# A cross-attention and mixed feed-forward layer on one core: residual and output sums of GpSimd made one step earlier, statistics and mix ahead of the query rounding on VectorE, query products behind both halves of the scores on TensorE

## The reference, cut to what matters

```python
# block 1: attention with 16 query heads of 16, one shared key/value head
xn = layernorm(x)
q  = (xn @ Wq + bq) -> 16 heads;  k = ctx @ Wk + bk;  v = ctx @ Wv + bv
p  = softmax(where(mask == 0, -1e9, q k^T / 4))
x1 = x + (p v) @ Wo + bo
# block 2: mix along the sequence, nine paths, one chosen per token
x2 = layernorm(x1)
xm = mk[0]*x2[s-1] + mk[1]*x2[s] + mk[2]*x2[s+1]
h  = xm @ W1[p] + b1[p]        (9 paths of 64);   gate = tanh(xm @ Wo1 + bo1) @ Wo2 + bo2
c  = (h[chosen] @ W2[chosen] + b2[chosen]),  chosen = argmax(gate)
out = x1 + layernorm(x2 + c) * gamma + beta
```

## Time and profile before

| what | us |
|---|---|
| median of 3 runs | 396.97 |
| lowest and highest of them | 395.99, 398.92 |
| the profiled execution | 397.85 |
| span of its instructions | 396.0 |
| TensorE busy | 335.4 |
| VectorE busy | 265.0 |
| GpSimd busy | 190.0 |
| ScalarE busy | 182.7 |

### The profile page before, as it was taken

The page is one execution under the profiler, slowest core; times in us unless marked ns, Lnnn a source line. Parts: engine busy times, 40 slices in busy tenths (PEclk is TensorE's granted clock), DMA queues, the critical chain, the costliest instruction groups (busy, mean ns, idle before and its releaser), DMA issues.

```text
span 396.0 us, 7447 instructions
## 1 busy us (share of the span) xinstructions
PE 335.4 (85%) x2764; PEld 245.9 (62%) x2764; DVE 265.0 (67%) x590; ACT 182.7 (46%) x285; POOL 190.0 (48%) x225
## 2 busy tenths in 40 slices
PE   1686884894999999898999999899999799979990
PEld 0563472373467956686577856685678376966890
DVE  2346296278177846897399638885678754698866
ACT  1432744435445456435645454445651555357400
POOL 0240106201807349562939277744954496339234
PEclk9998995898899999999999999999999999999996
DMA  8308000100020001200120003000100010001003
GB/s 218 129 0 196 27 2 14 54 0 2 0 68 3 0 2 55 66 2 0 53 66 0 0 13 104 2 0 2 55 0 2 0 55 2 0 2 54 2 2 106
DMA packets 20421, 13.46 MB, mean 34 GB/s; under 512 B 10081, under 2 KB 20138, under 8 KB 20394
## 3 DMA queue, kind: packets, MB, share of 16 engines
q1 hardware_dynamic: 18754, 12.53, 10.8%
q10 hardware_dynamic: 1640, 0.57, 0.6%
HBM read 8.90 MB, written 4.19 MB: 33 GB/s over the span
## 4 chain that ended last, share of the span: by engine, by line
PE 44%; DVE 21%; POOL 11%; issue 9%; ACT 8%; DMA 5%; ACTq 1%; DVEq 0%; POOLq 0%; SPq 0%
PE ps L419 8%; DVE mx L1085 5%; PE ps L527 3%; PE ps L572 3%; PE ps L424 3%; DVE st L1032 3%; ACT xh L848 3%; DMA xin<-in_x 3%; PE ps L637 3%; PE ps L562 3%; POOL x L1391 3%; POOL x1b L1397 3%; DVE osb L1103 2%; DVE x L1111 2%; PE ps L553 2%
## 5 line engine op out<-in xcount | busy, mean ns | idle before, releaser
L1371 POOL TENSOR_TENSOR rs<-ve,halfneg 128x4 f32<-128x4 f32 x24 | 25.1, 1046 | 148.8 <-DVE ve L1048 148.8
L823 ACT ACTIVATE e<-ps 128x1024 f32<-128x1024 f32 x32 | 31.1, 1023 | 35.8 <-PE ps L534 35.8
L1079 DVE CAST qr<-q 128x512 fp32r<-128x512 f32 x16 | 8.6, 540 | 47.8 <-ACT q L811 47.4
L1085 DVE TENSOR_REDUCE mx<-ps 128x16 f32<-128x1024 f32 x32 | 37.7, 1210 | 0.7 <-PE ps L502 0.7
L655 PE MATMUL ps<-w2h,hmh 128*128 128x256 f32 (+1 forms) x140 | 35.8, 291 | 0.0
L656 PE MATMUL ps<-w2l,hmh 128*128 128x256 f32 (+1 forms) x140 | 34.6, 282 | 0.0
L419 PE MATMUL ps<-xmh,w1h 128*128 128x512 f32 x80 | 27.5, 425 | 6.2 <-ACT hs L874 4.0
L572 PE MATMUL ps<-wo,osb 128*128 128x256 f32 x128 | 31.3, 390 | 1.6 <-DVE osb L1103 1.6
L874 ACT ACTIVATE hs<-ps,b1s 128x512 f32<-128x512 f32 x28 | 19.4, 692 | 25.5 <-PE ps L424 25.5
L1428 POOL TENSOR_TENSOR hml<-hs,hmh 128x512 fp32r<-128x512 f32 x24 | 29.9, 1271 | 1.5 <-ACT hmh L884 1.5
L1417 POOL TENSOR_TENSOR y<-xh2f,gms 128x256 f32<-128x256 f32 x28 | 21.0, 781 | 20.1 <-DVE xh2f L1057 20.1
(11 more groups left out here) (155 smaller groups left out, 825.0 us busy)
## 6 DMA issues: line engine op xcount, KB each, us to landing
xin<-in_x SPq DMA_DIRECT2D x8, 512.0 KB, 3.7
out<-y SPq DMA_DIRECT2D x7, 512.0 KB, 2.9
min_<-in_mask_Bx1xSxS_ik SPq DMA_DIRECT2D x8, 128.0 KB, 3.6
cst<-in_constants SPq DMA_DIRECT2D x1, 660.5 KB, 10.0
hs<-in_L_ffn_W SPq DMA_DIRECT2D x2, 288.0 KB
hs<-in_L_ffn_W SPq DMA_DIRECT2D x1, 512.0 KB
out<-xin SPq DMA_DIRECT2D x2, 256.0 KB, 2.2
cst<-in_constants SPq DMA_DIRECT2D x1, 384.0 KB, 6.5
```

The source lines that it names most:

```text
L823: nc.scalar.activation(e[:, 2 * i:2 * i + 2, :], ps[:, bank:bank + 2, :], ACT.Exp).then_inc(s_e, 1)
L1085: v.tensor_reduce(mx[:, k, :].rearrange("p (a h) -> p a h", a=2), ps[:, bank:bank + 2, :].rearrange("p a (h s) -> p a h s", s=SK), AX.X, A ...
```

## The change

On TensorE the products of path groups 0 and 4 go ahead of the second half of the scores, and the query products behind it. ScalarE does the exponentials in two parts with `hidden` 0 and 4 between, and applies layer norm 1 to `after` ahead of the copy of the products with the values. VectorE takes the statistics of `after` and the mix first in its step, and rounds the queries behind them. GpSimd makes x1 + beta for the next step's `f` and x + bo for the next step's `n` (which is this step's `front`) behind the low parts, and no longer at the start of the next step; `x1b` therefore has one buffer per half, and the low parts of the last half borrow `qr`. The SyncE queue has the same instructions in the same order.

```diff
@@ TensorE, step
                 if n:
                     scores_transposed(*n, 0, front)
+                if f:
+                    w1(*f, 0)
+                    w1(*f, 4)
+                    scores_transposed(*n, 1, front)
                 if front:
                     wq(*front, fb)
-                if n:
+                if n and not f:
                     scores_transposed(*n, 1, front)
                 if f:
-                    w1(*f, 0)
-                    w1(*f, 4)
                     w1(*f, 1)
                     gate(*f)
@@ ScalarE, step (softmax_exp now does two of its four parts at a call)
                 if n:
-                    softmax_exp(*n)
+                    softmax_exp(*n, 0)
+                if f:
+                    hidden(*f, 0)
+                    hidden(*f, 4)
+                if n:
+                    softmax_exp(*n, 1)
                 if front:
                     q_copy(*front, 0 if f else 6)
                 if f:
-                    hidden(*f, 0)
-                    hidden(*f, 4)
-                if f:
                     hidden(*f, 1)
-                if n:
-                    pv_copy(*n)
-                if f:
-                    hidden(*f, 2)
-                    hidden(*f, 3)
                 if f and f[1] == 0:
                     mixed_hi(f[0], 1)
                 if f and n[1] == NJ - 1:
                     early_mixed_hi(n[0])
+                if after and f:
+                    layernorm1_apply(*after)
+                if n:
+                    pv_copy(*n)
+                if f:
+                    hidden(*f, 2)
+                    hidden(*f, 3)
                     keep_xh2(*f)
...
-                if after:
+                if after and not f:
                     layernorm1_apply(*after)
@@ VectorE, last_column and step
                 dve.wait_ge(s_xm, at(b, NJ * KD, KD))
+                dve.wait_ge(s_earlyl, at(b, KD, KD))
                 v.tensor_copy(xmh[:, :, col], xm[:, :, col]).then_inc(s_xmh, KD)
                 dve.wait_ge(s_xmh, at(b, NJ * KD, KD))
-                dve.wait_ge(s_earlyl, at(b, KD, KD))
...
-                if front:
-                    q_round(*front)
+                if after and f:
+                    layernorm1_stats(*after)
                 if f and f[1] == 0:
                     second_mix(f[0])
                 if f and n[1] == NJ - 1:
                     early_mix(n[0])
+                if front:
+                    q_round(*front)
                 if f:
                     argmax(*f)
                 if n:
                     invert(*n)
-                if after and f:
-                    layernorm1_stats(*after)
@@ GpSimd, add_beta and step
-                pool.wait_ge(s_yo, 1 + at(b, NJ, j))
+                pool.wait_ge(s_yo, at(b, NJ, j))
                 for k in range(NT):
-                    a = g.tensor_tensor(x1b[:, k], x1[:, j, k], bts[:, :], ALU.add)
+                    a = g.tensor_tensor(x1b[:, j, k], x1[:, j, k], bts[:, :], ALU.add)
...
-            def step(n, front, f, after):
-                if f:
-                    add_beta(*f)
-                if n:
-                    add_bo(*n, f)
+            def step(n, front, f, after, next_f):
+
...
+                if next_f:
+                    add_beta(*next_f)
                 if n:
                     rstd2(*n)
+                if front:
+                    if not next_f:
+                        pool.wait_ge(s_wo_in, 32)
+                    add_bo(*front, next_f)
```

More of the change, by code:

```diff
@@ L681, in step @@
                     w1(*f, 4)
+                    scores_transposed(*n, 1, front)
+                if front:
+                    wq(*front, fb)
+                if n and not f:
+                    scores_transposed(*n, 1, front)
+                if f:
                     w1(*f, 1)
@@ L816, in maxima, with softmax_exp @@
                 nc.scalar.activation(nmT[:, :], bf16_bank(bank), ACT.Copy).then_inc(s_nT, 1)
-            def softmax_exp(b, j):
+            def softmax_exp(b, j, half):
                 act.wait_ge(s_dn, at(b, NJ, j))
-                for i in range(4):
+                for i in (2 * half, 2 * half + 1):
                     act.wait_ge(s_st, at(b, NJ * NPAIR, j * NPAIR + 2 * i + 2))
```

37 lines of the change are left out of this document (16 added, 21 removed).

## The result

| kernel | median us | lowest, highest | runs |
|---|---|---|---|
| before | 396.94 | 395.99, 398.92 | 4 |
| after | 430.06 | 429.07, 432.51 | 4 |

The changed kernel takes 1.084 times as long, with a 95% interval of 1.077 to 1.090. The forecast was 426.4 us, range 413 to 438. The profiled execution of the changed kernel took 429.56 us, of which the span is 427.8 us.

A forecast was written before the change was run, and what follows sets the result against it. TensorE, busy 85% of the span, was taken as the bound. Profiled 397.85 us + 31.8 for three late steps - 2.4 won = 427.3, less 0.9 to the median's scale: 426.4 us, range 413 to 438.

The forecast's parts named there:

- late step: B1, A2 and B2, where the load of x stands behind a store: 10.6 us each, 31.8 us in all.
- mix: VectorE's mix without GpSimd's sums beside it, only a power and one low part: taken as 4.3 us, from 5.98 and 4.02.
- value products later than before: TensorE's products with the values wait for the casts until S+21.8, not S+13.28: 8.5 us later.
- clock: TensorE's granted clock falls to 0.50 behind each long stop: 2.5 us lost per stop, bounds 1.3 and 2.75.
- from path product 2 to the next step: Behind the value products, TensorE's 0.40 us wait for the normalised products (`osb`) goes: -0.4 us.
- half of the overlap with the store: Load of x lands between S+12.9 alone and S+15.2 wholly behind the store; half the difference taken, S+14.0.
- lower bound of 1.3: Least clock loss per TensorE stop, in us, since part of the small value products is not bound by the clock.
- The gains: TensorE's filled holes: 0.8 us in C, 0.4 in A1, 1.2 in D; sum -2.4 us, bounds 0 and -4.5.
- rival 1: x lands by S+3.7, casts end about S+13, steps shorten by 6.8 us in all: 390.2 us; chance 0.06.
- Rival 2: Casts don't hold the value products; TensorE first waits at the selectors, 3.2 us in three steps: 404.2 us; chance 0.02.
- Rival 3: Filled TensorE holes and a late x cancel, with x landing by about S+6: 397 us; chance 0.03.
- rival 4: Same mechanism, larger: x at S+15.2, mix 5.98, casts 1.60, clock 2.75, 14.8 us per step: 441.5 us; no separate chance.

The follow-up runs named there:

- e1: The changed kernel with SyncE's queue issuing each load of x ahead of the store that stood before it: 396.24 us, ratio 0.998 to the kernel before.
- e3: The changed kernel with the statistics back behind `invert` and ScalarE's layer norm 1 back behind `selected_hi`, queue as in the change: 391.85 us, ratio 0.986.
- e2: The changed kernel without the value products' wait for the rounded queries, the load of x as late as in the change: 418.70 us, ratio 1.053.
- e10: The kernel before with VectorE's new order alone, statistics and mix ahead of the casts: 450.55 us, ratio 1.132.
- e5: The changed kernel with loads ahead of stores and without the value products' wait for the rounded queries: 390.79 us, ratio 0.985 to the kernel before.
- e7: The changed kernel with loads ahead of stores, statistics back, and no wait for the rounded queries at the value products: 391.37 us, ratio 0.986.
- e8: The changed kernel with statistics back and casts ahead of the mix, so VectorE's list is the one of before: 391.28 us, ratio 0.987.
- e12: The changed kernel with 46 idle products on TensorE in the stop of the B steps only: 425.48 us, ratio 1.072 to the kernel before.
- e4: The kernel before with the change's TensorE order, ScalarE's exponentials in two parts and the wait in `last_column`: 393.45 us, ratio 0.990.
- e9: The kernel before with GpSimd's part alone (x1 + beta and x + bo a step earlier) and `last_column`'s changed wait: 400.71 us, ratio 1.010.
- e11: The changed kernel with 36 idle products on TensorE ahead of the value products, in A1 too: 433.71 us, ratio 1.092 to the kernel before.

## Why the prediction was right, and where its sizes were off

The steps by their own order, from S in each late step:

| step of the prediction | forecast | B1 | A2 | B2 |
|---|---|---|---|---|
| store goes out | 8.63 | 8.99 | 8.70 | 8.98 |
| load goes out | 9.2 | 9.75 | 9.70 | 9.70 |
| x has landed, statistics start | 14.0 | 14.86 | 13.84 | 14.18 |
| statistics and mask | 2.57 | 2.48 | 2.48 | 2.48 |
| mix | 4.3 | 4.90 | 4.91 | 4.90 |
| casts | 0.9 | 0.75 | 0.75 | 0.75 |
| casts end | 21.8 | 22.91 | 21.91 | 22.24 |
| value products later than before | 8.5 | 9.74 | 8.72 | 9.07 |
| clock | 2.5 | 1.99 | 2.59 | 2.86 |
| from path product 2 to the next step | -0.4 | -0.68 | +0.37 | -0.62 |
| a late step | 10.6 | 11.05 | 11.68 | 11.31 |

The three lines above the last add up to it in every step; the three steps are 34.04 us, where 31.8 were forecast.

**The mechanism** is shown link by link. The load behind the store: e1 moves it and 34 us go. The list of VectorE behind the load: e3 leaves the load late and moves the statistics, and 38 us go. The value products behind the casts: e2 takes that wait away and they run at S+12.2. The number of late steps, three and not four, came out as read from the queue: B1, A2, B2.

One rule of the Trainium skill was weighed on this point. "DMA: Bandwidth & Descriptors", on the anatomy of one DMA, has the issuing sequencer wait before dispatch; from that the prediction drew that a blocked store holds what is behind it. The runs agree: the load of B1 goes out at 150.45, behind the store at 149.69, in the change, and at 141.18, before the step, where it stands ahead of the store (e1).

**The sizes.** The value products stood at S+13.28 in A2 and S+13.27 in B1 and B2 before, and stand at S+23.01, 22.00 and 22.34 in B1, A2 and B2 now; the forecast was S+21.8. The load was issued 0.5 us later than forecast, since y came up to 0.4 us later and the queue's two issues stand 0.7 to 1.0 us apart, not 0.56. It then took 5.1, 4.1 and 4.5 us, where half of the overlap with the store had given 4.8; over the whole kernel loads take a median of 4.3 us and stores 3.3, 0.6 and 0.4 more than in the earlier trace rows:

```profile
xin<-in_x SPq DMA_DIRECT2D x8, 512.0 KB, 4.3
out<-y SPq DMA_DIRECT2D x7, 512.0 KB, 3.3
```

The mix took 0.6 us more than 4.3, and this is the term that was too small in every step. Its first five instructions run at their free speed; the last takes 1.63 us beside one low part of GpSimd's. In e10, where no low part stands beside it, the whole mix takes 4.02 us. The prediction had seen that low part coming and gave it 0.3 us; it cost 0.9. The clock term of 2.5 us is met in the mean of the three steps, 2.48, and in none by itself; B2's 2.86 lies above the bound of 2.75 that was given. The lower bound of 1.3 had its reason wrong: the small value products went from 1.92 to 3.64 us, nearly double, so hardly a part of them is free of the clock. Behind path product 2 the wait for `osb` is gone (0.72 us in B1 and B2, 0.40 in A2), and in B1 and B2 another of 0.6 us at a selector, but TensorE waits anew for x1 ahead of line 513 (0.34 us) and 0.2 us longer ahead of the transposes t2.

**The gains.** The forecast had 2.4 us outside the late steps: 0.4 in A1, 0.8 in C, 1.2 in D. The profile shows 0.13 lost in A1, 0.37 won in C and 0.6 in D and the tail, together 0.8. Two reasons show, and why C wins only half of its 0.8 does not. In A1 the path products now wait 1.05 us, at S+4.15, for the last column (`xmh`, line 1158), which itself waits for GpSimd's low part; the prediction had named this neighbour and left it between 0 and 0.8. And the tail of this execution has a slow stretch behind its wait for the last column that other executions of the same code don't have: D and the tail take 84.6 us here and 83.0 to 83.1 in e5, e7, e8 and e12 (see the hardware below). Without it the three gains are -0.13, 0.37 and 2.2 us, and their sum of 2.4 meets the forecast by luck. The holes were filled, but a step's length does not follow a hole in front of path product 1: e4, which does nothing else, gains 0.16 us in A1 and 0.01 in A2, where the 0.79 us hole of the earlier trace rows was. What the edits of the change are worth together, when nothing is late, is e5's 6.7 us (397.48 - 390.79), near the 6.8 of rival 1, though it is made up otherwise: 1.75, 0.69 and 1.69 us in B1, A2 and B2, and 2.2 in D and the tail.

**The total.** The median lies 3.7 us above the forecast, and not one term alone is the reason. The three late steps hold 2.2 us more, the gains 1.6 less, the start phase 1.4 less by itself, and 1.4 come from where the two profiled executions lie among their runs: 0.9 above the median before, 0.5 below it after.

**GpSimd** took the sums without harm, as forecast. The second layer norm's power and x + bo at the end of A1:

```profile
134.74 1.02 POOL L1375 TENSOR_TENSOR rs<-ve,halfneg 128x4 f32<-128x4 f32 x1 [2.57 <-DVE ve L1052]
136.02 2.80 POOL L1395 TENSOR_TENSOR x<-xin,bos 128x256 f32<-128x256 f32 x4
```

This power still waits 2.57 us for VectorE, and the third layer norm's, behind x + bo at 139.63, waits 0.82. And x + bo takes 2.80 us there, not the 3.87 that it took in A2 before, where VectorE was at work beside it.

**The rivals.** Rival 1 (x in time, 390.2 us) is what e5 measured, 390.8; its condition was false in the change, and by one instruction's place in a queue. e1 adds a correction: x in time alone does not reach it, because the casts end at S+13.4 and not at S+13, and the wait in `pv` still bites by 0.4 to 1.2 us. Rival 2 (the casts don't hold the value products, 404 us) had the wrong next wait and so too small a price: e2 has the condition and takes 418.7. I had looked for the selectors, 3.2 us late and no stop for the clock; the slot of the gate's products came first, with 5.48 us and the slow clock. Rival 3 needed x by about S+6, and it landed at S+13.8 to S+14.9. Of rival 4's four slow terms the clock's 2.75 was reached in B2, and the landing at S+15.2 nearly so in B1 (S+14.86); the slow mix and casts were not met.

**What stays open.** The falls of the clock behind short waits, in e9, e1 and the changed kernel's tail, were measured and not traced to a cause. Whether TensorE's part keeps 2.6 or 3.8 us is not settled: the start phase and the one slow stretch of the tail are as large as the difference. Leaving the load where it is and issuing it from another engine's queue was not tried; that would separate the queue from the DMA engines' share, which e1 does not, as it also moves the load away from the store.

## What to carry to other kernels

Before a consumer of a load is moved ahead in an engine's list, read when the load is issued, not when its buffer is free: in one queue a load waits for every store ahead of it, and a store waits for its data. In a list that an engine takes in order, put what depends on the latest arrival behind what other engines wait for (e3: the statistics back behind `invert`, 38 us). And when such a chain is found, mend the first link: the same edits with the load ahead of the store, and without a wait that a later one repeats, run in 390.8 us (e5), and with the statistics left in place in 391.3 to 391.9 (e8, e3), all about 1.4% faster than the kernel before (ratios 0.985 to 0.987, every interval below 1).

## What the runs showed of the hardware

**The same stop with and without a fall of the clock.** In e1 TensorE runs the same products in the same times ahead of a stop of 1.24 us in B1 and in B2. The windows before and after it, B1 first, then B2 (columns as above):

```profile
151.00:155.20 4.20, 4.20 (x23) 3.30 (x21) 4.09 (x5) 3.20 (x6) 4.20 (x5) 1.00 0.37 126
```

```profile
237.33:241.60 4.27, 4.27 (x23) 3.31 (x21) 4.16 (x5) 3.27 (x6) 4.27 (x5) 1.00 0.36 123
```

```profile
156.50:160.00 3.50, 3.49 (x20) 0.99 (x24) 2.75 (x6) 2.08 (x4) 2.42 (x2) 0.52 0.02 5
242.80:246.30 3.50, 3.45 (x80) 2.34 (x80) 2.82 (x6) 3.01 (x5) 2.48 (x3) 1.00 0.00 0
```

```profile
156.51 3.57 PE L554 MATMUL ps<-e,vd 128*32 128x512 f32 x16 [1.24 <-issue]
...
242.85 1.92 PE L554 MATMUL ps<-e,vd 128*32 128x512 f32 x16 [1.24 <-issue]
```

Ahead of it the clock is 1.00 both times. Behind it it is 0.52, the 1.2 GHz level, in B1, and the value products take 3.57 us; in B2 it stays at 1.00 and they take 1.92. The step lengths differ by 1.84 us, 44.53 and 42.69, where e5's B1 and B2, without such a stop, differ by 0.20. What tells the two apart no row shows, so a stop of this length has no fixed price here: between 1.24 and 2.9 us.

The tail has such a place too: with GpSimd's part of the change in it, TensorE stops there 1.61 us for `xmh`. The changed kernel, then e5:

```profile
379.02 0.87 PE L419 MATMUL ps<-xmh,w1h 128*128 128x512 f32 x2 [1.61 <-DVE xmh L1158]
379.69 1.05 PE L419 MATMUL ps<-xmh,w1l 128*128 128x512 f32 x2
...
341.93 0.70 PE L426 MATMUL ps<-xmh,w1h 128*128 128x512 f32 x2 [1.61 <-DVE xmh L1164]
342.47 0.63 PE L426 MATMUL ps<-xmh,w1l 128*128 128x512 f32 x2
```

The first products behind it are slow in the changed kernel, in e1, e2, e3, e9 and e11, and at full speed in e5, e7, e8 and e12 (in the kernel before the stop is 2.21 us and they are fast, in e4 2.20 and they are slow); for the changed kernel and e12, whose code is the same there, D and the tail take 84.6 and 83.1 us. So some 1.5 us of any comparison of two profiles here can be this one stop. Nor has a long stop one price: the clock cost 2.0, 2.6 and 2.9 us behind stops of 10.7, 9.7 and 10.1 us in one execution. A clock term is best read from the products that run behind the stop, in each step.

**VectorE beside GpSimd.** One instruction of the mix, TENSOR_SCALAR on 128x511, takes 0.48 us alone and 0.95 beside GpSimd's making of y in e5. There even a TENSOR_TENSOR on 36 elements, 0.20 us in e3 while GpSimd is idle, takes 0.99 and 1.22 beside two low parts of 1.27 us each, while a TENSOR_REDUCE on as many elements, just ahead of them and beside the same low part, keeps its 0.19 (VectorE and GpSimd of e5, then VectorE of e3):

```profile
155.34 0.19 DVE L1183 TENSOR_REDUCE gmax<-gs 128x4 f32<-128x36 f32 x1
155.56 0.99 DVE L1190 TENSOR_TENSOR cand<-gs,gmax 128x36 f32<-128x36 f32 x1
156.59 1.22 DVE L1192 TENSOR_TENSOR gs<-cand,cst 128x36 f32<-128x36 f32 x1
```

```profile
155.22 2.53 POOL L1420 TENSOR_TENSOR xml<-xm,xmh 128x511 fp32r<-128x511 f32 x2
```

```profile
154.64 0.20 DVE L1182 TENSOR_TENSOR cand<-gs,gmax 128x36 f32<-128x36 f32 x1
```

The two long TENSOR_TENSORs end, at 156.55 and 157.81, where GpSimd's two low parts end (about 156.5 and 157.75). So in these rows a small TENSOR_TENSOR beside GpSimd lasts until GpSimd's instruction under way is over, whatever its own size, and the reduction of one operand does not.
